# One attention stage reordered: turns of q and k ahead of the v projections, k turned in the fourth bank, third norms ahead of the fourth squares, clip against a constant tensor

## What is computed

```python
h = shift_token(x)
qkv = h @ wqkv                                  # 128 -> 3 * 512 channels, 8 heads of 64
q, k, v = jnp.split(qkv, 3, axis=-1)
q = l2norm(q) * qs                              # t / clip(norm(t), 1e-12), per head
k = l2norm(k) * ksc
q, k = rotary_xpos(q, k)                        # tables of cos and sin, with a scale
o = local_attention(q, k, v)                    # windows of 64, own and preceding window, softmax
x = x + o @ wo
```

## Time and profile before

| | before |
|---|---|
| median of 3 runs | 4148.99 us (4142.99 to 4150.77) |
| the profiled execution | 4157.49 us, span 4155.7 us |
| granted clock of TensorE, mean | 0.905 of full speed |
| PE busy | 3285.2 us (79%) |
| PE weight loads busy | 1929.7 us (46%) |
| DVE busy | 2552.8 us (61%) |
| ACT busy | 2603.5 us (63%) |
| POOL busy | 1726.6 us (42%) |
| DMA engines | 5 GB/s on average |

### The profile page before, as it was taken

The page is one execution under the profiler, slowest core; times in us unless marked ns, Lnnn a source line. Parts: engine busy times, 40 slices in busy tenths (PEclk is TensorE's granted clock), DMA queues, the critical chain, the costliest instruction groups (busy, mean ns, idle before and its releaser), DMA issues.

```text
span 4155.7 us, 57708 instructions
## 1 busy us (share of the span) xinstructions
PE 3285.2 (79%) x17248; PEld 1929.7 (46%) x17248; DVE 2552.8 (61%) x4239; ACT 2603.5 (63%) x5871; POOL 1726.6 (42%) x1428
## 2 busy tenths in 40 slices
PE   4688878877788878887887788787887887888787
PEld 2354444544444444444544445445444544455443
DVE  5575766657556565666647666575666656666443
ACT  4466667665676656667666676656767566676554
POOL 2353343524435353343533535344353533535332
PEclk9798999999999999998989999989999899989898
DMA  2000000000000000000000000000000000000000
GB/s 83 3 1 1 6 1 6 1 1 7 1 7 1 1 7 1 7 1 1 6 1 7 1 7 1 1 7 1 7 1 1 7 1 7 1 1 3 1 3 3
DMA packets 18444, 21.03 MB, mean 5 GB/s; under 512 B 769, under 2 KB 17153, under 8 KB 17793
## 3 DMA queue, kind: packets, MB, share of 16 engines
q1 hardware_dynamic: 18048, 16.44, 1.2%
HBM read 12.24 MB, written 4.19 MB: 4 GB/s over the span
## 4 chain that ended last, share of the span: by engine, by line
PE 45%; DVE 20%; ACT 13%; issue 12%; POOL 9%; DMA 0%; DVEq 0%; POOLq 0%; ACTq 0%; SPq 0%
PE bank L564 8%; PE bank L626 5%; POOL hc L1464 4%; PE bank L813 3%; DVE tmp L1375 3%; DVE hst L1235 3%; PE bank L797 3%; PE bank L746 3%; POOL Pm L1537 2%; PE bank L547 2%; PE bank L532 2%; PE bank L773 2%; DVE tmp L1370 2%; DVE bank L1227 2%; PE bank L756 2%
## 5 line engine op out<-in xcount | busy, mean ns | idle before, releaser
L1464 POOL TENSOR_TENSOR hc<-hst,Cs 128x512 f32<-128x512 f32 x512 | 655.4, 1280 | 967.5 <-DVE hst L1235 957.2
L1235 DVE TENSOR_TENSOR_SCAN hst<-dA,bank 128x512 f32<-128x512 f32 x512 | 625.0, 1221 | 133.5 <-issue 58.9
L564 PE MATMUL bank<-W,xs 128*128 128x512 f32 x960 | 493.7, 660 | 25.5 <-DVE tmp L1375 23.8
L1537 POOL TENSOR_TENSOR Pm<-Pm,rinv 128x512 f32<-128x512 f32 x256 | 271.5, 1060 | 455.8 <-DVE rinv L1395 438.5
L927 ACT COPY Cs<-bank 128x512 f32<-128x512 f32 x512 | 299.3, 585 | 247.2 <-PE bank L547 217.4
L1227 DVE TENSOR_TENSOR bank<-u,bank 128x512 f32<-128x512 f32 x512 | 351.3, 686 | 158.7 <-PE bank L547 154.6
L547 PE MATMUL bank<-parts,sel 96*128 96x512 bf16 x1024 | 356.9, 423 | 107.8 <-DVE hst L1235 42.0
L1522 POOL TENSOR_TENSOR oT<-tmp 128x512 f32<-128x512 f32 x256 | 325.0, 1269 | 247.0 <-DVE tmp L1375 184.3
L921 ACT ACTIVATE dA<-delta,neg_a 128x512 f32<-128x512 f32 x512 | 372.6, 728 | 67.8 <-DVE hst L1235 67.1
L532 PE MATMUL bank<-C,hc 128*128 128x128 f32 x2048 | 353.6, 302 | 35.5 <-POOL hc L1464 35.5
L1054 ACT ACTIVATE Pm<-bank,mx 128x128 f32<-128x128 f32 x1024 | 366.7, 387 | 16.3 <-DVE mx L1389 14.7
(11 more groups left out here) (224 smaller groups left out, 6197.0 us busy)
## 6 DMA issues: line engine op xcount, KB each, us to landing
W<-wpack SPq DMA_DIRECT2D x1, 4498.0 KB, 13.3
x_tok<-x SPq DMA_DIRECT2D x16, 256.0 KB, 2.9
out<-xa SPq DMA_DIRECT2D x16, 256.0 KB, 2.2
rot<-tables SPq DMA_DIRECT2D x2, 512.0 KB, 15.9
wc_f<-taps SPq DMA_DIRECT2D x1, 1024.0 KB, 19.2
C<-cpack SPq DMA_DIRECT2D x1, 721.0 KB, 14.5
Pm<-mask SPq DMA_DIRECT2D x1, 320.0 KB, 14.8
tmp<-rowpack SPq DMA_DIRECT2D x1, 256.0 KB, 17.1
```

The lines of the kernel that those rows point to most:

```text
L564: mm(b[:, :], weights, rhs, start=True, stop=True).then_inc(full(ring, job), 1)
L1235: v.tensor_tensor_scan(o, a, b, 0.0, ALU.mult, ALU.add).then_inc(sem("a_h"), 1)
L1464: g_.tensor_tensor(hc[:, k % 2, :], hst[:, k % 2, :], Cs[:, k % 2, :], ALU.mult)\
L1537: g_.tensor_tensor(windows, windows, over(rinv[:, k % 2, :], P), ALU.mult).then_inc(sem("t_P"), 1)
```

## The change

- In `B_JOBS`, in PE's queue and in ACT's queue, the turns of q and k (and their copies) come ahead of the v projections (and their copies) of the same slot. This matters in slots 2 and 3, where both exist.
- k is always turned in the fourth bank, q of tiles 2 and 3 in bank 2. The banks become: qt0 0, kt0 3, v05 1, v06 3, q03 2, k03 0, qt1 1, kt1 3, v07 2, qt2 2, kt2 3, S0 0, qt3 2, kt3 3, S1 1. So qt0 waits for the copy of v03, kt0 for that of v04, v05 for the sin products of q02, v06 for the copy of kt0, q03 for the sin products of k02, k03 for the copies of qt0, qt1 for the copy of v05, kt1 for that of v06, v07 for the sin products of q03, qt2 for the copy of v07, kt2 for that of kt1, scores 0 for the sin products of k03, qt3 for the copies of qt2, kt3 for the copy of kt2, scores 1 for the copies of qt1.
- `weigh(0)` also waits for the last copy of k, since the fourth bank is `o_acc`.
- ACT takes the norms of tiles 2 and 3 at the start of slots 3 and 4, ahead of the squares of tile 3; those of tiles 0 and 1 stay behind the squares.
- The clip, a tensor_scalar with 1e-24, becomes a tensor_tensor with a tensor `least` of that value (one memset more in the setup).

```diff
@@ B_JOBS
         if _s < NT:
             B_JOBS += [(f"q{_l}{_s}", "t_sin", ...), (f"k{_l}{_s}", "t_sin", ...)]
-            B_JOBS += [(f"v{_l}{_w}", "t_v", 7 * _l + _w) for _w in (2 * _s + 1, 2 * _s + 2) if _w < NW]
         if 2 <= _s < 2 + NT:
             B_JOBS += [(f"qt{_l}{_s - 2}", "t_q", 8 * _l + 2 * _s - 2), (f"kt{_l}{_s - 2}", "t_k", 4 * _l + _s - 1)]
+        if _s < NT:
+            B_JOBS += [(f"v{_l}{_w}", "t_v", 7 * _l + _w) for _w in (2 * _s + 1, 2 * _s + 2) if _w < NW]
@@ HOME
+HOME |= {f"qt{l}{s}": 2 for l in range(NL) for s in (2, 3)}
+HOME |= {f"kt{l}{s}": OUT for l in range(NL) for s in range(NT)}
@@ sbuf
+        least = sb("least", [2, HA])
@@ PE, project
                             norm_sum("B", f"{kind}{l}{s}", i, xsh[:, s * P:(s + 1) * P], w(f"w{kind}{l}"))
+
+                    def project_v(s):
                         for at in (2 * s + 1, 2 * s + 2):
@@ PE, weigh
-                        if g == 0:
-                            pe.wait_ge(*step("t_v", i, 7 * l + (3 if half == 0 else 7)))
+                        if n > 0 and g == 0:
+                            pe.wait_ge(*step("t_v", i, 7 * l + 7))
                         if n == 0:
                             pe.wait_ge(*step("t_v", i, 7 * l + 6))
+                            pe.wait_ge(*step("t_k", i, 4 * l + 4))
@@ PE, slots
                         if 2 <= s < 2 + NT:
                             channel_major(s - 2)
+                        if s < NT:
+                            project_v(s)
@@ ACT, slots
+                        if s in (NT - 1, NT):
+                            act.wait_ge(*step("t_clip", i, 4 * l + s))
+                            f(rqk[:, s - 1], ssq[:, s - 1], ACT.Ln).then_inc(sem("t_rln"), 1)
+                            act.wait_ge(*step("t_rln", i, 4 * l + s))
+                            f(rqk[:, s - 1], rqk[:, s - 1], ACT.Exp, scale=-0.5).then_inc(sem("t_r"), 1)
                         if s < NT:
                             ...  # squares of q and k
-                        if 1 <= s <= NT:
+                        if s in (1, 2):
                             ...  # the same norms
-                        if s < NT:
-                            ...  # copies of v
                         if 2 <= s < 2 + NT:
                             ...  # copies of qt and kt
+                        if s < NT:
+                            ...  # copies of v
@@ DVE, setup and clip
+            done(v.memset(least[:, :, :], 1e-24))
-                            v.tensor_scalar(ssq[:, s], ssq[:, s], 1e-24, None, ALU.max).then_inc(sem("t_clip"), 1)
+                            v.tensor_tensor(ssq[:, s], ssq[:, s], least[:, :, :], ALU.max).then_inc(sem("t_clip"), 1)
```

More of the change, by code:

```diff
@@ L1044, in stage_b @@
                                 .then_inc(sem("t_k"), 1)
+                        if s < NT:
+                            for at in (2 * s + 1, 2 * s + 2):
+                                if at < NW:
+                                    act.wait_ge(*filled("B", f"v{l}{at}", i))
+                                    b = bank("B", f"v{l}{at}")
+                                    nc.scalar.copy(vt[:, at - 1, :], b[:, :]).then_inc(sem("t_v"), 1)
                         if 1 <= n < NU + 1:
@@ L1543, in _ @@
             run(pool, prologue, scan, head, stage_b, finish)
-SETUP = 7 + 4 + 3 + 2 + TAPS + 1 + 2 + len(TABLES) * NL
+SETUP = 1 + 7 + 4 + 3 + 2 + TAPS + 1 + 2 + len(TABLES) * NL
 def shape_constants():
```

## The result

| | before | after |
|---|---|---|
| median | 4149.33 us (4 runs) | 4042.1 us (4037.67 to 4044.44, 4 runs) |
| ratio to before | | 0.9745, 95% interval 0.973 to 0.9761 |
| span of the profiled execution | 4155.7 us | 4041.4 us |
| granted clock of TensorE, mean | 0.905 | 0.919 |

A forecast was written before the change was run, and what follows sets the result against it. The prediction took a chain of waits through all four compute engines as the bound. It summed 32 layers at 3.15 us to 101 us, giving 4048 us (chance 0.58, own range 4010 to 4080; wider range 4000 to 4150).

The forecast's parts named there:

- the first exponentials are the link that counts: Attention layers: everything later in the layer hangs on the first exponentials, so their start is the measure of the change.
- At nothing: DVE's clip: the tensor_tensor waits for POOL's instruction as the tensor_scalar does, so the edit gains nothing.
- The 1.24 us of POOL in layer 0: Layer 0, tile 2: with its norms early, POOL starts scaling at 2044.94 and not 2046.18, 1.24 us earlier.
- the sign that the prediction named: POOL's wait for the norms (L1026) was to fall from 116 us to under 50.
- the turns of q0 and k0 that come early: Layer 0, PE: q0 and k0 turned right after k02, at about 2036.3, ahead of v05 and v06.
- The argument on scores 0: Layer 0, PE: scores 0 wait for k03's sin products, not kt2's copy; about 2050.5 and not 2052.87.
- the walk: Link-by-link times to the first exponentials: 3.35 us earlier in layer 0 (3.75 before a low-clock deduction), 3.4 in layer 1.
- The 3.15 taken for each layer: Gain per attention layer, below 3.35 and 3.4 since the squeezed scan should keep a few tenths; 101 us over 32.
- Only PE's lateness goes: Rival, chance 0.2: POOL gains nothing; 3.75 us for two layers, 60 us in all, 4089 us.
- The slower rival: Rival, chance 0.1: v05 and v06 hold up the scan at a low clock; 1.0 us per layer lost, 4181 us.
- The rival of a shorter clip: Rival, chance 0.05: the clip on DVE does get shorter, 71 to 77 us more gain, about 3975 us.
- Given back within the layer: Rival, chance 0.07: something else, such as the scan, paces the eight units, so no gain: 4149 us.

The follow-up runs named there:

- the reduce: Clip as tensor_reduce over pairs (sum, 1e-24), one SBUF input: 4129.9 us, ratio 0.9935 in the kernel before; 4051.59 and 4052.29 us in the changed kernel.

## Why the prediction was right, and where it was not

**The measure.** That the first exponentials are the link that counts is borne out for the whole change: in the mean over 14 sequences (2 to 15 for layer 0, 1 to 14 for layer 1), worked out from the starts of L1370 before and L1385 after, the length from one layer's first product to the next one's fell by 4.5 us for layer 0 (91.8 to 87.4) and 2.6 for layer 1 (160.1 to 157.6), with exponentials 3.7 and 2.5 us earlier. That is 7.0 us per sequence, and 16 x 7.0 = 112, against the 114.3 us between the two spans and the 107 between the medians. It is not the whole measure: from the first exponentials of layer 0 to the first product of layer 1 it is 60.5 us before, 59.8 after, 58.7 in banks alone and 60.7 in banks and norms (means, one profile each), though these last two start the exponentials alike. No experiment asked what sets that stretch.

**The clip.** At nothing: right, shown by the clip alone. The Trainium skill, "SBUF — State Buffer", section "Who interferes with whom", says that a DVE instruction with two SBUF inputs contends with a GpSimd instruction that reads SBUF; the median of 756 ns beside POOL, for 174 ns at the least, agrees. The same section of the Trainium skill says that tensor_reduce never contends on trn2; the reduce's 185 to 188 ns in all its instances agree.

**The norms.** The 1.24 us of POOL in layer 0 came as forecast, also alone. But POOL's wait for the norms did not fall under 50 us, the sign that the prediction named; it is 69.7, since in layer 1 it does not go. And the prediction did not say that the norms matter mostly because the new order delays the squares: with the new banks and the old order POOL's wait is gone in layer 0 without them, and they are worth about 7 us (0.9757 to 0.9728), at the edge of what the runs tell.

**Turns and banks.** The sum was right, the credit was not. The prediction treated order and banks as one edit, and began its walk with the turns of q0 and k0 that come early. In the runs the new order costs 110 us alone and brings nothing with banks and norms. The gain comes from the banks: scores 0 and 1, kt0, q03 and kt3 start or wait by other readers. Which of these waits carries how much no run separates. The argument on scores 0 and the reader of its bank was the part that held, and it needs no new order. That a sum built on the early turns came within 6 us of the measured gain is in part luck.

**The sum.** Layer 0 was put at 3.35 by the walk, which took 0.4 off for a low clock while v05 and v06 run, and measured 3.7 in the median. Both cases occur. Of the 15 layers 0 with a scan beside them, 8 keep the full clock and start the exponentials at 27.4 us; in the other 7 the granted clock is 0.57 to 0.64 from 12 to 16 us, and they start at 27.5 to 28.2, 0.5 later in the mean.

Layer 1 was put at 3.4, and measured 2.9 in the median and 2.5 in the mean: that term was too large. The walk had POOL's wait for the norms gone. In all 15 sequences POOL still waits 0.80 us before it scales tile 3. Before tile 2 it waits 0.6 us in 9 of them, with the exponentials at 27.7 to 28.0 us, and 1.7 us in the other 6, with the exponentials at 29.0 to 29.7; the granted clock from 12 to 20 us is 0.79 in the nine and 0.57 in the six. (The walk also has v05 and v06 end at 2135.9, where its own 1.53 us each from 2132.4 give 2135.5; that slip makes the gain smaller, not larger.) The 3.15 taken for each layer hid the error of layer 1.

A part of layer 1's gain, 0.4 us in the mean, is given back before the next sequence's layer 0: the Mamba block's product with its output weights (L706 after, L702 before) runs at the low clock more often, and takes 41.2 us in all against 34.6. In the sequence shown it took, for the same four matmuls, after and then before:

```profile
1967.64 3.17 PE L706 MATMUL bank<-PT,W 128*128 128x512 f32 x4
```

```profile
2023.27 1.88 PE L702 MATMUL bank<-PT,W 128*128 128x512 f32 x4
```

**The rivals.** "Only PE's lateness goes" was put at 4089 us; turns and banks without norms, the kernel nearest to it, had 4102. The slower rival was real with the old banks, where the order costs 110 us, and in part with the new ones and the norms in their old place, where it costs 48. With the new banks v05 waits for q02 rather than k02. The rival of a shorter clip did not occur, and its price was too high: with the wait taken away by the reduce the gain was 21 us in the kernel before, and none in the changed one. "Given back within the layer" did not happen: in layer 0 the projection of the attention's output starts 3.8 us earlier. The signs besides that of POOL's wait came about as named: the clip's median, PE's wait for a copy of k, and, in the sequence shown, 9.9 and 8.8 us from the first product of tile 3 to the first exponentials, where 10 and 8 were named.

## What to carry to other kernels

When an edit mixes an order and a place, walk each alone: here two lines that say which bank a job takes are nearly the whole gain, and the order that came with them is a loss without them and, with them, costs nothing only once the norms are moved. For every wait on a buffer ask whose reader it is; a job that takes the bank of a late reader holds up all that stands behind it in an in-order queue, other chains' work included. And a part that is worth nothing alone can be worth half of the change beside another, so what is taken apart has to be tried in both surroundings.

## What the runs showed of the hardware

A 16-element tensor_tensor on DVE with two SBUF inputs, begun beside POOL, takes as long as POOL's current instruction needs to end (medians of 756 to 898 ns for 174 at the least), and so does the tensor_scalar (768). In the kernel before, 112 of the 128 clips begin while POOL is in an instruction, and each ends within 0.12 us of that instruction's end, 30 ns after it in the median; the other 16 take 174 to 177 ns. In the changed kernel all 128 begin beside a busy POOL and end so. This is worked out from the starts and ends in the traces. A tensor_reduce of twice the input took 185 to 188 ns in all of its 128 instances, POOL busy or not.

And work that became shorter on DVE made the kernel slower by 13 us, with TensorE's granted clock down from 0.920 to 0.908 and its low level of 1.2 GHz at 24 to 30 us after the first product of layer 0 where it had been at 12 to 16. The two go together; that the clock is the cause of the 13 us is not shown. In the kernel with the new banks, the old order and the norms of tile 0 moved as well, the same edit gained 24 us; which of these differences decides no run separates.
